# Cross-attention with split fp32 operands: the softmax weights' lower halves and the reciprocal root on GpSimd, and a straight list for VectorE

## What is computed

```
memory_proj = ctx @ W_mem.T
scores = x @ memory_proj.T / sqrt(512)
attn = softmax(scores, axis=-1)
memory_context = attn @ memory_proj
gate = sigmoid(concat(x, memory_context) @ W_gate.T + b_gate)
fused = x + gate * memory_context
out = fused * rsqrt(mean(fused**2, -1) + 1e-6) * norm_w
```

## Time and profile before

| | |
|---|---|
| median of 3 runs | 561.93 us (561.55 to 562.57) |
| the profiled execution, by its own time | 561.31 us |
| its span in the profile | 559.5 us |
| busy: TensorE matmul / weight load | 538.0 us (96%) / 436.4 us (78%) |
| busy: VectorE / ScalarE / GpSimd | 503.5 (90%) / 335.7 (60%) / 134.0 us (24%) |
| mean granted TensorE clock | 0.994 |
| DMA | 54.25 MB, mean 97 GB/s |

### The profile page before, as it was taken

One profiled execution on the slowest core, in us unless ns is written; L12 is line 12 of the kernel. 1 busy time (PEld: TensorE's weight loads), 2 busy tenths in 40 slices (PEclk: granted clock), 3 DMA queues, 4 the chain that ended last, 5 costly groups with the idle time before them and its releaser, 6 DMA issues.

```text
span 559.5 us, 8972 instructions
## 1 busy us (share of the span) xinstructions
PE 538.0 (96%) x2416; PEld 436.4 (78%) x2416; DVE 503.5 (90%) x847; ACT 335.7 (60%) x633; POOL 134.0 (24%) x102
## 2 busy tenths in 40 slices
PE   6999999999999999999999999999999999999992
PEld 5877888878888788878888788887888778887881
DVE  3789859999899998899988998999988999889976
ACT  4666636665567655586366764766556754657534
POOL 0005500244002530055101550024400351005600
PEclk9999999999999999999999999999999999999997
DMA  9974362511684107821276115752078311210033
GB/s 224 261 130 68 95 107 77 100 63 34 141 174 107 37 23 154 170 75 37 89 142 135 56 37 123 164 100 73 0 159 178 85 37 69 69 38 21 0 115 112
DMA packets 184338, 54.25 MB, mean 97 GB/s; under 512 B 161528, under 2 KB 174848, under 8 KB 184320
## 3 DMA queue, kind: packets, MB, share of 16 engines
q1 hardware_dynamic: 183792, 53.52, 41.2%
q10 hardware_dynamic: 528, 0.52, 0.3%
HBM read 45.63 MB, written 8.39 MB: 97 GB/s over the span
## 4 chain that ended last, share of the span: by engine, by line
PE 65%; DVE 19%; issue 10%; ACT 2%; SPq 2%; DMA 1%; ACTq 0%; DVEq 0%
PE bank L355 14%; PE bank L357 13%; PE bank L356 13%; PE bank L516 7%; PE bank L517 7%; PE bank L518 7%; DVE p_lo L830 6%; DVE s L871 3%; DVE fused L976 2%; DVE fused L983 2%; DVE gate L897 2%; ACT fused L688 2%; DVE gate L926 2%; SPq L239 2%; DMA x_raw<-in_x_dram 1%
## 5 line engine op out<-in xcount | busy, mean ns | idle before, releaser
L1147 POOL TENSOR_TENSOR psum_rows<-psum_rows,p_tmp 128x512 f32<-128x512 f32 (+1 forms) x88 | 122.4, 1391 | 86.5 <-ACT p_tmp L665 85.4
L830 DVE TENSOR_TENSOR p_lo<-p_tmp,p_hi 128x512 fp32r<-128x512 f32 (+1 forms) x104 | 92.2, 888 | 4.8 <-ACT p_hi L627 4.8
L665 ACT ACTIVATE p_tmp<-s 128x512 f32<-128x512 f32 (+1 forms) x104 | 65.2, 627 | 45.1 <-DVE s L871 44.4
L1147 POOL TENSOR_TENSOR psum_rows<-p_tmp 128x512 f32<-128x512 f32 x8 | 10.8, 1352 | 309.0 <-ACT p_tmp L665 309.0
L355 PE MATMUL bank<-q_hi,mt_hi 128*128 128x512 f32 (+1 forms) x208 | 81.8, 393 | 0.0
L516 PE MATMUL bank<-p_hi,mem_hi 128*128 128x512 f32 (+1 forms) x208 | 81.2, 390 | 0.1
L356 PE MATMUL bank<-q_lo,mt_hi 128*128 128x512 f32 (+1 forms) x208 | 81.2, 390 | 0.0
L357 PE MATMUL bank<-q_hi,mt_lo 128*128 128x512 f32 (+1 forms) x208 | 81.2, 390 | 0.0
L517 PE MATMUL bank<-p_lo,mem_hi 128*128 128x512 f32 (+1 forms) x208 | 81.1, 390 | 0.0
L518 PE MATMUL bank<-p_hi,mem_lo 128*128 128x512 f32 (+1 forms) x208 | 81.0, 389 | 0.0
L627 ACT ACTIVATE s<-bank 128x512 f32<-128x512 f32 (+1 forms) x104 | 62.0, 596 | 19.4 <-PE bank L357 18.9
(11 more groups left out here) (91 smaller groups left out, 1028.4 us busy)
## 6 DMA issues: line engine op xcount, KB each, us to landing
mem_raw<-in_ctx_dram SPq DMA_DIRECT2D x48, 256.0 KB, 3.0
mem_blocks<-in_ctx_dram SPq DMA_DIRECT2D x64, 136.0 KB
...
```

The source lines that it names most:

```text
L665: nc.scalar.activation(p_tmp[0:r, t % TMP_RING, :], s[0:r, t, :], ACT.Exp, scale=float(D) ** -0.5).then_inc(exp_done, 1)
L830: return nc.vector.tensor_tensor(dst, src, hi.bitcast(F32), ALU.subtract)
L1147: nc.gpsimd.tensor_tensor(psum_rows[0:r, :], a, p_tmp[0:r, t % TMP_RING, :], ALU.add).then_inc(p_added, 1)
```

## The change

GpSimd gets two things more. `p_lo_part(t)`, the same subtraction with the same waits, stands behind each `add_p(t)` in its list. `rms(b - 1)` becomes three GpSimd operations of 128x4, a multiply, an add and a `pow` with -0.5, behind tile 8 (`RMS_AT`), and behind the last batch for the end; VectorE and ScalarE wait for `rms_done` where they used the result.

VectorE's list of a batch becomes a straight one. The 13 shifts no longer wait for the weights behind them; `gate_input`, `gate_ctx` and `add_x` of b - 1 stand between the first seven, `add_bias(0)` behind shift 6, the first two transposes of x and `add_bias(1)` behind shift 8, `add_bias(2)` behind shift 11, `add_bias(3)` behind shift 12. Then come `mem_lo_part(6)`, the other transposes and the `xt_lo_part`s, the wait for `rms_done` and the outputs. In the first batch all 13 shifts stand ahead of `add_bias(0)`, and two transposes of x ahead of `add_bias(1)`. ScalarE's list keeps its tiles in order; `tanh`, `copy_ctx`, `squares` and `xt_hi_part` stand behind other tiles (`TANH_AT`, `COPY_AT`, `SQUARES_AT`, `X_AT`). TensorE's and SP's lists stay.

```diff
-        X_AT = [6, 7, 9, 10]
-
-        X_BLOCKS_AT = [4, 5, 7, 8]
-        MEM_BLOCKS_AT = [10, 11]
-
         QUERY_AT = 9
 
-        ADD_AT = [1, 3, 11]
+        TANH_AT, COPY_AT, SQUARES_AT = [0, 3, 4], [1, 3, 5], [3, 5, 6, 7]
+
+        X_AT = [8, 9, 10, 11]
+
+        RMS_AT = 8
 
 
         SPLIT_BY_SCORES = {0: [0], 2: [1], 4: [2], 5: [3], 6: [4, 5]}
-        SPLIT_BY_SOFTMAX = {5: [6]}
+        SPLIT_BY_SOFTMAX = [6]
+        SPLIT_AT = 5
...
-                    for t in range(MT + 1):
-                        for q in SPLIT_BY_SOFTMAX.get(t, []):
-                            mem_hi_part(b, q, first)
-                        softmax(b, t, first)
-                        if t == 1:
-                            weights(V[1])
-                        if not last and t - 1 in X_AT:
-                            xt_hi_part(b + 1, X_AT.index(t - 1), False)
-                        if not last and t == 12:
-                            q_hi_part(b + 1, 0)
-                            q_hi_part(b + 1, 1)
                 else:
                     tanh(b - 1, 0)
                     copy_ctx(b - 1, 0)
-                    tanh(b - 1, 1)
-                    for t in range(MT + 1):
-                        for q in SPLIT_BY_SOFTMAX.get(t, []):
+                for t in range(MT + 1):
+                    softmax(b, t, first)
+                    if first and t == 1:
+                        weights(V[1])
+                    if not first:
+                        if t in TANH_AT:
+                            tanh(b - 1, TANH_AT.index(t) + 1)
+                        if t in COPY_AT:
+                            copy_ctx(b - 1, COPY_AT.index(t) + 1)
+                        if t in SQUARES_AT:
+                            squares(b - 1, SQUARES_AT.index(t))
+                    if t == SPLIT_AT:
+                        for q in SPLIT_BY_SOFTMAX:
                             mem_hi_part(b, q, first)
-                        softmax(b, t, first)
-                        if t in (0, 2, 3):
-                            copy_ctx(b - 1, max(t, 1))
-                        if t in (2, 3):
-                            tanh(b - 1, t)
-                        if t == 1:
-                            squares(b - 1, 0)
-                        if t - 2 in ADD_AT:
-                            squares(b - 1, ADD_AT.index(t - 2) + 1)
-                        if not last and t - 1 in X_AT:
-                            xt_hi_part(b + 1, X_AT.index(t - 1), False)
-                        if not last and t == 13:
-                            q_hi_part(b + 1, 0)
-                            q_hi_part(b + 1, 1)
+                    if not last and t in X_AT:
+                        xt_hi_part(b + 1, X_AT.index(t), False)
+                if not last:
+                    q_hi_part(b + 1, 0)
+                    q_hi_part(b + 1, 1)
...
-            def p_lo_part(b, t):
-
-                dve.wait_ge(p_has_hi, MT * b + t + 1)
-                if t >= LO_RING:
-
-                    dve.wait_ge(pe_u, MT * b + t - LO_RING + 1)
-                r = rows(t)
-                lo_part(p_lo[0:r, t % LO_RING, :], p_tmp[0:r, t % TMP_RING, :], p_hi[0:r, t, :]).then_inc(p_has_lo, 1)
-
-            def softmax(b, t, with_x):
-
-                if t + 3 < MT:
-                    shift(b, t + 3)
-                if with_x and t in X_AT:
-                    xt_lo_part(b + 1, X_AT.index(t))
-                p_lo_part(b, t)
...
+                elif k == 0:
+
+                    dve.wait_ge(ctx_copied, NT * (b - 1))
...
+                    if p == 0:
+
+                        dve.wait_ge(z_done, NT * (b - 1))
+                    else:
 
...
-            def transpose_next(b, t, first):
-                if t in X_BLOCKS_AT:
-                    if t == X_BLOCKS_AT[0]:
-                        if first:
-
-                            dve.wait_ge(wt_split_lo, 8)
-                        else:
-
-                            dve.wait_ge(ctx_copied, NT * b)
-                    transpose_x(b + 1, X_BLOCKS_AT.index(t))
-                if t in MEM_BLOCKS_AT:
-                    if t == MEM_BLOCKS_AT[0] and not first:
-
-                        dve.wait_ge(z_done, NT * b)
-                    transpose_mem(b + 1, MEM_BLOCKS_AT.index(t))
...
-            def rms(b):
-
-                count = [NEWTON_OPS * b]
-
-                def link(instruction):
-
-                    count[0] = count[0] + 1
-                    instruction.then_inc(newton, 1)
-                    dve.wait_ge(newton, count[0])
-
-
-                dve.wait_ge(squares_done, NT * (b + 1))
-                link(nc.vector.tensor_scalar(mean_sq[:, :], sq_sum[:, :], 1.0 / D, EPS, ALU.mult, ALU.add))
-                link(nc.vector.tensor_scalar(r_rms[:, :].bitcast(I32), mean_sq[:, :].bitcast(I32), -0.5, RSQRT_MAGIC,
-                                             ALU.mult, ALU.add))
-                for _ in range(NEWTON_STEPS):
-                    link(nc.vector.tensor_tensor(nw_a[:, :], r_rms[:, :], mean_sq[:, :], ALU.mult))
-                    link(nc.vector.scalar_tensor_tensor(nw_b[:, :], nw_a[:, :], -0.5, r_rms[:, :], ALU.mult, ALU.mult))
-                    link(nc.vector.scalar_tensor_tensor(r_rms[:, :], nw_b[:, :], 1.5, r_rms[:, :], ALU.add, ALU.mult))
...
-                    shift(b, 0)
-                    shift(b, 1)
-                    shift(b, 2)
-                    for t in range(MT):
-                        for q in SPLIT_BY_SOFTMAX.get(t, []):
-                            mem_lo_part(b, q)
-                        softmax(b, t, not last)
-                        if t == 1:
-                            weights(V[1])
-                        if 1 <= t < 1 + NT:
-                            add_bias(b, t - 1, first)
-                        transpose_next(b, t, first)
+                    for t in range(6):
+                        shift(b, t)
+                    weights(V[1])
+                    for t in range(6, MT):
+                        shift(b, t)
+                    add_bias(b, 0, first)
+                    transpose_x(b + 1, 0)
+                    transpose_x(b + 1, 1)
+                    for j in range(1, NT):
+                        add_bias(b, j, first)
                 else:
                     reciprocal(b - 1)
                     gate_input(b - 1, 0)
                     reduce_max(b, first)
+                    gate_input(b - 1, 1)
+                    shift(b, 0)
                     gate_ctx(b - 1, 0)
-                    gate_input(b - 1, 1)
+                    shift(b, 1)
                     add_x(b - 1, 0)
-                    shift(b, 0)
-                    shift(b, 1)
                     shift(b, 2)
-                    for t in range(MT):
-
-                        if t in (1, 2):
-                            gate_input(b - 1, t + 1)
-                        if 3 <= t < 3 + NT:
-                            add_bias(b, t - 3, first)
-                        if t in (0, 2, 4):
-                            gate_ctx(b - 1, 1 + t // 2)
-                        if t in ADD_AT:
-                            add_x(b - 1, ADD_AT.index(t) + 1)
-                        for q in SPLIT_BY_SOFTMAX.get(t, []):
-                            mem_lo_part(b, q)
-                        softmax(b, t, not last)
-                        if not last:
-                            transpose_next(b, t, first)
-                    rms(b - 1)
+                    gate_input(b - 1, 2)
+                    gate_ctx(b - 1, 1)
+                    shift(b, 3)
+                    add_x(b - 1, 1)
+                    gate_input(b - 1, 3)
+                    gate_ctx(b - 1, 2)
+                    shift(b, 4)
+                    add_x(b - 1, 2)
+                    shift(b, 5)
+                    gate_ctx(b - 1, 3)
+                    add_x(b - 1, 3)
+                    shift(b, 6)
+                    add_bias(b, 0, first)
+                    shift(b, 7)
+                    shift(b, 8)
+                    if not last:
+                        transpose_x(b + 1, 0)
+                        transpose_x(b + 1, 1)
+                    add_bias(b, 1, first)
+                    shift(b, 9)
+                    shift(b, 10)
+                    shift(b, 11)
+                    add_bias(b, 2, first)
+                    shift(b, 12)
+                    add_bias(b, 3, first)
+                for q in SPLIT_BY_SOFTMAX:
+                    mem_lo_part(b, q)
+                if not last:
+                    xt_lo_part(b + 1, 0)
+                    transpose_x(b + 1, 2)
+                    xt_lo_part(b + 1, 1)
+                    transpose_x(b + 1, 3)
+                    transpose_mem(b + 1, 0)
+                    xt_lo_part(b + 1, 2)
+                    transpose_mem(b + 1, 1)
+                    xt_lo_part(b + 1, 3)
+                if not first:
+
+                    dve.wait_ge(rms_done, b)
                     for j in range(NT):
```

(42 more changed lines are left out.)

14 lines of the change are left out of this document (6 added, 8 removed).

## The result

The changed kernel takes **620.06 us** (median of 4 runs, 617.66 to 620.68) against 562.01 (4 runs, 561.55 to 562.57): ratio **1.1033**, 95% interval 1.102 to 1.1046. 627 (600 to 647) was forecast. The profiled execution took 620.26, its span 618.5.

What follows compares the result with a forecast made beforehand. TensorE was taken to bound the kernel. First batch 7.7, six batches of 8.4, last batch 8.2, end -1.0 sum to +65.3 us; on 561.9 that gives 627 us, range 600 to 647.

Steps and rivals of the forecast that it cites:

- The bound and the mechanism: TensorE binds; late add_bias on VectorE leaves it idle before gate_x(2) of batches 1 to 7, 6 to 7 us each.
- The schedule by hand: VectorE's new list, delayed by GpSimd and copy_ctx, ends add_bias 0 at 255.08 against 248.46: +6.0 us a batch.
- Rival 2: At gate_x: TensorE's stall comes but its clock does not fall, 609 us; chance 0.16.
- The clock: TensorE's clock falls to half rate in the pause before gate_x(2), slowing matmuls behind it: +2.4 us a batch.
- "half" of the 24 matmuls: Clock loss in gate_x(2) and (3) taken as 2.7 us, half the 5.4 if all 24 ran at the lower level.
- First batch, last batch, end: Outside the six loop batches: first batch +7.7 us, last batch +8.2, ScalarE's wait for the root at the end -1.0.
- Rival 1: VectorE loses little to GpSimd's lock; list and copy_ctx waits cost +2.1 us a batch: 581 us; chance 0.11.
- no clock loss: In the 581 us case, TensorE's clock was to stay up despite add_bias being late by +2.1 us a batch.
- Rival 3: GpSimd itself becomes the bound, if a subtraction takes 2.0 us instead of 1.29: near 657 us; chance 0.05.
- 4 to 5 us of room at tile 9: Slack GpSimd was thought to have at tile 9 before its lower halves would be late for TensorE.
- Rival 4: Faster: TensorE's 1.48 us of waits at gate_x go in 7 batches, -10.4, with 1.0 at the end: 551 us; chance 0.04.

Runs made afterwards that it cites:

- e10: The changed kernel with add_bias early in VectorE's list and GpSimd's additions and subtractions on 32 of 512 columns: 550.1 us.
- e9: The changed kernel with GpSimd's additions and subtractions on 32 of 512 columns and 14 filler matmuls ahead of gate_x(2) from batch 1 on: 582.71 us.
- e3: The changed kernel with 26 matmuls whose result nobody uses ahead of gate_x(2) in each batch but the first, filling TensorE's pause: 609.87 us.
- e1: The changed kernel with add_bias 0 ahead of add_x 2, add_bias 1 behind shift 5, and the other two one place earlier: 595.12 us.
- e2: The changed kernel, lists as they are, with GpSimd's additions and subtractions on 32 of 512 columns: 594.06 us.
- e4: The kernel before the change with add_bias one tile earlier, nothing else: 559.6 us against 562.2.

## Why the prediction was right, and where it was not

The runs make a chain from a kernel without the three burdens to the kernel after:

| run | what it has | us | step |
|---|---|---|---|
| e10 | new lists, early `add_bias`, narrow GpSimd | 550.1 | |
| e9 | + `add_bias` where the change puts it | 582.7 | +32.6 |
| e3 | + GpSimd's full work | 609.9 | +27.2 |
| after | + the clock behind the pause | 620.1 | +10.2 |

The kernel before, at 562.0, stands 12 above the first line. Of the 32.6 us, 8.0 fall in the first batch (105.4 against 97.4), where the transposes of x change place too. GpSimd's full work with early `add_bias` is e1 less e10, 45 us with its clock loss: moving `add_bias` hides part of GpSimd's price and GpSimd's hides part of the order's, so the shares hold in this order only.

- **The bound and the mechanism: right.** TensorE, idle in one piece before `gate_x(2)`, ended by `add_bias`: 6.4 us in each of batches 1 to 7 (6 to 7 forecast).
- **The schedule by hand: right.** `add_bias(0)` 19.06 us behind `gate_input(1)`, 19.3 forecast; +5.65 us a batch without the clock (e3), 6.0 forecast. Operations that meet GpSimd took 1.18 to 1.68 us, the four outputs 6.5 (7 forecast), the subtraction 1.29 undisturbed, the root's three operations 1.6 from the first start to the last end. Rival 2's 609 was this case without the clock, and e3 gives 609.9; that they meet so closely is in part luck, since e3's batches are 0.35 shorter than forecast, its last batch is 1.2 longer and its end holds 1.5 us of clock.
- **The clock: the term that was over-sized**, "half" of the 24 matmuls. For batches 1 to 7 the terms were 6 x 2.4 + 2.7 = 17.1 us; measured were 10.2 (11.3 batch by batch). In the six batches of the loop the clock took 1.66 us each on average, where 2.4 was forecast, and the rest of the list 5.65, where 6.0 was: together 6.5 of the 6.9 us by which 627 was too high. In the batch shown above some 12.5 matmuls ran at the lower level, `weighted(0)` came 8.2 us behind `gate_x(2)` (5.9 in e3), and the size was nearly right; in every other batch it is less. The timeline of the next batch, with the same pause:

```profile
351.04 0.80 PE L353 MATMUL bank<-wg1t_hi,xt_hi 128*128 128x512 f32 x1 [6.42 <-DVE gate L868]
...
354.55 0.39 PE L355 MATMUL bank<-wg1t_hi,xt_lo 128*128 128x512 f32 x1
354.78 0.39 PE L353 MATMUL bank<-wg1t_hi,xt_hi 128*128 128x512 f32 x1
```

  Its windows read 0.90 in 346 to 348 and 0.50 in 348 to 350, so the clock fell earlier in the pause than above (0.98 in 274 to 276), and it was back earlier, by 354.5, after some 7.5 matmuls. So it costs 1.2 in this batch and 2.2 in the other. By the Trainium skill, "TensorE: Matmul & The Clock Gate", Part 1, an idle engine drops to half rate and gets the full rate back after sustained work: the traces of after agree on both.
- **First batch, last batch, end: right in their sums.** +7.9, +8.0, -0.8 against 7.7, 8.2 and -1.0, the first with its longest wait before `gate_x(3)`, for x. In the last batch luck helped: by e3 its list costs 6.7 and not 5.5, its clock 1.3 and not 2.7. TensorE's timeline of after in the first batch, which answers to the earlier trace rows:

```profile
53.00 0.50 PE L353 MATMUL bank<-wg1t_hi,xt_hi 128*128 128x512 f32 x1 [1.02 <-DVE gate L868]
60.52 0.50 PE L353 MATMUL bank<-wg1t_hi,xt_hi 128*128 128x512 f32 x1 [4.51 <-DVE gate L868]
```

  At the end ScalarE still stands 1.75 us behind the root where it stood 2.27; 1.2 was forecast, since `pow` was unknown. ScalarE's timeline of after:

```profile
613.42 1.33 ACT L811 ACTIVATE fused<-gate,r_rms 128x512 f32<-128x512 f32 x2 [1.75 <-POOL r_rms L1128]
```

- **Rival 1** (581, the order alone) is e9: 582.7 with 2.0 us a batch, 2.1 forecast. The lists' own waits for `copy_ctx` do that. Its "no clock loss" was wrong: e2, which differs from e9 only in that the pause isn't filled, takes 594.1.
- **Rival 3** (GpSimd the bound) didn't come, but the argument was thin: the "4 to 5 us of room at tile 9" were made by TensorE's own pause. Without it (e1) GpSimd is 2.7 us late at tile 9.
- **Rival 4** (faster, 551) is e10 to within a microsecond, and shows what it takes: the order mended and GpSimd's work gone.
- Not foreseen: in the kernel before, taking away the wait at `gate_x` alone gains 2.6 us and not 10.4 (e4), because VectorE is late at its next readers too.

How VectorE's meeting with GpSimd and GpSimd's own lateness divide the 27 us, no run separates, since both went together in the narrow runs; but the traces tell it for this order. TensorE's waits in e3:

```profile
PE bank L353 <- DVE gate L872: 9.1, 9, 3.6
...
PE bank L514 <- POOL p_lo L1122: 0.9, 1, 0.9
```

With GpSimd's full work TensorE waits for GpSimd once, 0.9 us in the last batch; everywhere else behind the start it waits for `add_bias`. And `add_bias(0)` is 3.5 us later in after than in e2, because the six `gate_ctx` and `add_x` ahead of it take 4.5 us longer there, of which 0.95 comes back in shorter waits for `copy_ctx`. The batches of e3 are 3.6 longer than those of e9, and seven times that is 25 of the 27 us. So with `add_bias` where the change puts it, nearly all of it is VectorE's meeting with GpSimd. With `add_bias` early (e1) the waits are for GpSimd instead; how the 45 us divide there stays open.
